# The opening of a recurrence and feed-forward layer kernel, rearranged: decay's row loaded alone ahead of x, clip logarithms on GpSimd, w2's absolute sums in halves, idle products ahead of x

## The chip, the cores and the metric

The kernel runs on one core of one Trainium2 chip. The metric is the device time of one execution in microseconds (us). The kernel before takes 821.13 us, the median of three runs (821.13, 821.13 and 821.78). Lower is better.

## The reference, cut to what matters

```python
def _L0_attn_ref(x, Wr, Wk, Wv, Wo, decay, ln_w):
    r = jax.nn.sigmoid(jnp.einsum('btd,ed->bte', x, Wr))
    k = jnp.einsum('btd,ed->bte', x, Wk)
    v = jnp.einsum('btd,ed->bte', x, Wv)
    log_decay = jnp.log(jnp.clip(jax.nn.sigmoid(decay), 1e-07))
    scale = jnp.exp(t * log_decay[None, :])               # t = 0 .. T-1
    cum = jnp.cumsum(k * v / jnp.clip(scale, 1e-10)[None], axis=1)
    y = _rmsnorm(r * cum * scale[None], ln_w)
    return jnp.einsum('btd,ed->bte', y, Wo)

def _L0_ffn_ref(x, w1, b1, w2, b2):                        # binarized: mean(|w|, axis=1) * sign(w)
    h = jax.nn.gelu(jnp.einsum('bsd,hd->bsh', x, bw1) + b1, approximate=False)
    return jnp.einsum('bsh,dh->bsd', h, bw2) + b2

x = _layernorm(x + _L0_attn_ref(x, ...))
x = _layernorm(x + _L0_ffn_ref(x, ...))                    # x: (8, 2048, 256), D = 256, H = 1024
```

## The kernel before

The 8 sequences of 2048 tokens are cut into 32 chunks of 512 tokens. A chunk passes through a pipeline of stages: x is scaled and split into two fp16 halves (xh on ACT, xl on DVE); R makes the products for k, v and r on PE (12 products of 512 columns for one half of the channels, one m at a time: m = 0 is k, 1 is v, 2 is r); kvs on DVE turns k and v into `kvg`; scans runs the recurrence along time and multiplies by r into `y`; ysq on ACT squares y, ysqs on GpSimd (POOL in the rows) adds the squares, block_sums on DVE and sum_rows on PE bring them to mean squares (mean_sq), and GpSimd takes the root (root_rms). yh and yl split y, O multiplies by Wo, residual1, ustats and norm1 make the first norm, F1 and gelu make the hidden layer, hh and hl split it (four pairs of 128-column blocks of the hidden layer in the first chunk), F2 makes the last product, and zmul, zadd, zstats and norm2 finish.

Five engines run five programs, each in the order in which its code is written, and meet at semaphores. Nothing is scheduled by a planner. Each program is a setup, a prologue and a loop. The loop runs the chunks; while PE does F2 of chunk i, the others prepare chunks i+1 to i+3. The setup and the prologue (the opening, up to the first F2 at about 58 us of the trace) prepare weights and bring the first chunks to their places in the pipeline. Only the opening is touched by the change.

What the opening does for the change:

- The DMA queue of SP loads the rows of decay, ln_w and b1 into one tile `rows` (L271 to L273), then x of chunk 0, the three projection weights, x of chunk 1, Wo, w1, w2 and more. PE transposes `rows` to columns (L556), DVE copies them (L1090), ACT takes the sigmoid and the logarithm of decay.
- The clip table `clip_g` holds, for each channel and time step, the factor that the clip at 1e-10 leaves: exp(min(t log d + 23.03, 0)). It is made in four parts of 512 steps. Parts 0 and 1: a product and a minimum on DVE (clip_logs, L1107) and an exponential on ACT (clip_table, L746). Parts 2 and 3: a rectified product on ACT (clip_excess, L734) and an exponential on ACT (L748).
- Weight scales: DVE takes the largest absolute value of a weight (proj_maximum, L1074), PE sums it over partitions (L480), DVE makes the scale (L1079, L1080), ACT splits the high half (proj_split_hi, L726), DVE the low half (proj_split_lo, L1084).
- The hidden layer's scale needs the sums of |w1| (alphas1, L766); the factor of the output needs the sums of |w2| (alphas2, L773), which DVE scales (L1173), GpSimd spreads over a diagonal (diagonal, L1316) and PE turns into a row (alpha2_to_row, L531).
- PE has a helper idle_products (L457): transposes of the identity whose result nobody reads.

## Time and profile before

| | |
|---|---|
| median of 3 runs | 821.13 us |
| the profiled execution's own time | 821.11 us |
| its span in the trace | 819.3 us |
| PE busy (matmul) | 798.8 us, 97% |
| DVE busy | 771.3 us, 94% |
| ACT busy | 679.9 us, 83% |
| POOL busy | 295.3 us, 36% |
| chain that ended last, by engine | PE 88%, DVE 4%, POOL 2%, ACT 2%, issue 2% |

The span is counted from the first record on the core. Between the profiled execution's time and its span lie 1.8 us, which the trace does not divide. A busy share is that of the whole span; the opening is 8% of it and has its own limits, so it is read from the timelines of the engines, in order of time, where a row says when an operation began, how long it took, and how long its engine was idle before it and who ended that.

### The profile page before, as it was taken

To read this page: it belongs to the slowest core of one execution; us is meant where nothing else is said; L and a number is where in the kernel's file an instruction comes from. 1 tells how busy PE (TensorE), PEld (TensorE's weight loads), DVE (VectorE), ACT (ScalarE), POOL (GpSimd) and SP (SyncE) were. 2 spreads that over 40 slices of the span, in tenths; PEclk is the share of its full clock that TensorE was granted. 3 is DMA by queue.
4 is the path that set the end of the run, shared out by engine and by line. 5 is a ranking of instruction groups with operands and counts; after the bars stand their busy time and mean duration, and the time that the engine had idled before them with its cause. 6 is when DMAs were issued, how large, how long until landed. Compare 5 with 4: busy or idle time off the path is not lost.

```text
span 819.3 us, 16575 instructions
## 1 busy us (share of the span) xinstructions
PE 798.8 (97%) x5174; PEld 505.7 (62%) x5174; DVE 771.3 (94%) x1472; ACT 679.9 (83%) x973; POOL 295.3 (36%) x572
## 2 busy tenths in 40 slices
PE   6989999999999999999999999999999999999986
PEld 4555666656666656666656666655666665666654
DVE  7998999999999999999999999999999999999887
ACT  7987888888888888888888888888888888887775
POOL 3343323344223344333344333344333334332344
PEclk9999999999999999999999999999999999999999
DMA  8513553434553434553434454444454344444313
GB/s 261 99 27 78 129 125 84 110 94 102 128 128 86 115 81 105 125 128 92 113 79 109 118 128 100 105 89 106 112 128 105 100 97 104 106 102 104 78 26 104
DMA packets 168286, 86.27 MB, mean 105 GB/s; under 512 B 128572, under 2 KB 163912, under 8 KB 168264
## 3 DMA queue, kind: packets, MB, share of 16 engines
q1 hardware_dynamic: 147288, 52.97, 27.5%
q0 software_dynamic: 4608, 16.78, 10.4%
q10 hardware_dynamic: 16368, 16.25, 5.6%
q8 instruction: 11, 0.18, 0.1%
q14 instruction: 11, 0.09, 0.0%
HBM read 20.45 MB, written 16.78 MB: 45 GB/s over the span
## 4 chain that ended last, share of the span: by engine, by line
PE 88%; DVE 4%; POOL 2%; ACT 2%; issue 2%; DMA 0%; SPq 0%; POOLq 0%; DVEq 0%; ACTq 0%
PE ps_r L375 28%; PE ps_o L496 26%; PE ps_f L446 19%; PE ps_r L446 6%; PE ps_o L401 6%; PE ps_o L406 3%; DVE hid_lo L1008 1%; DVE u L959 1%; ACT hid L678 1%; DVE u_st L967 0%; PE ps_s L383 0%; DMA x_in<-in_L_attn_x_dram 0%; POOL root L1322 0%; POOL y_sqs L1310 0%; DVE state L923 0%
## 5 line engine op out<-in xcount | busy, mean ns | idle before, releaser
L496 PE MATMUL ps_o<-w2T,hid_hi 128*128 128x256 f16 x992 | 218.9, 273 | 3.4 <-DVE hid_lo L1008 3.0
L496 PE MATMUL ps_o<-w2T,hid_lo 128*128 128x256 f16 x992 | 218.8, 272 | 0.0
L375 PE MATMUL ps_r<-x_t,proj_hi 128*128 128x512 f16 x768 | 197.1, 379 | 1.2 <-issue 0.7
L446 PE MATMUL ps_f<-x_t,w1T 128*128 128x512 f16 x768 | 181.7, 379 | 1.6 <-DVE x_t L992 1.3
L678 ACT ACTIVATE hid<-ps_f,rows_c,f_scale 128x512 f32<-128x512 f32 x192 | 145.2, 774 | 42.2 <-PE ps_f L446 37.1
L1008 DVE SCALAR_TENSOR_TENSOR hid_lo<-hid,hid_scale,hid_hi 128x1024 f16<-128x1024 f32 (+1 forms) x136 | 160.3, 1222 | 0.9 <-POOL hid_hi L1343 0.6
L1310 POOL TENSOR_TENSOR y_sqs<-y_sq 128x512 f32<-128x512 f32 x32 | 46.7, 1459 | 309.6 <-ACT y_sq L653 309.6
L375 PEld LDWEIGHTS ps_r<-x_t,proj_hi 128*128 128x128 f16 x768 | 74.7, 98 | 91.3 <-issue 2.8
L713 ACT ACTIVATE hid_hi<-hid,hid_scale 128x2048 f16<-128x2048 f32 (+2 forms) x72 | 127.9, 1778 | 3.2
L446 PEld LDWEIGHTS ps_f<-x_t,w1T 128*128 128x128 f16 x768 | 74.9, 98 | 79.7 <-issue 1.6
L375 PE MATMUL ps_r<-x_t,proj_lo 128*128 128x512 f16 x384 | 114.2, 379 | 0.2 <-DVE proj_lo L1084 0.2
L496 PEld LDWEIGHTS ps_o<-w2T,hid_hi 128*128 128x128 f16 x992 | 97.0, 98 | 20.2 <-DVE hid_lo L1008 5.9
L496 PEld LDWEIGHTS ps_o<-w2T,hid_lo 128*128 128x128 f16 x992 | 97.1, 98 | 14.4
L647 ACT ACTIVATE r_tanh<-ps_r,x_scl 128x512 f32<-128x512 f32 x64 | 43.9, 686 | 32.6 <-PE ps_r L375 29.4
L653 ACT ACTIVATE y_sq<-y 128x512 f32<-128x512 f32 x62 | 39.1, 630 | 37.0 <-ACT res L707 15.9
L446 PE MATMUL ps_r<-x_t,w1T 128*128 128x512 f16 x256 | 69.6, 378 | 0.0
L707 ACT ACTIVATE res<-res,z_shift,z_rstd 128x256 f32<-128x256 f32 x126 | 65.1, 589 | 4.8 <-POOL z_shift L1356 2.6
L1322 POOL TENSOR_TENSOR root<-ms,neg_half 128x4 f32<-128x4 f32 x32 | 32.8, 1024 | 93.0 <-DVE ms L949 93.0
L375 PEld LDWEIGHTS ps_r<-x_t,proj_lo 128*128 128x128 f16 x384 | 37.5, 98 | 45.7 <-DVE proj_lo L1084 0.9
L696 ACT ACTIVATE res<-u,u_shift,u_rstd 128x256 f32<-128x256 f32 x120 | 61.9, 588 | 1.7 <-POOL u_shift L1338 1.7
L923 DVE TENSOR_TENSOR_SCAN state<-decay_f,state,kvg 128x512 f32<-128x512 f32 x48 | 61.5, 1281 | 0.8
L401 PE MATMUL ps_o<-wo_lo,y_hi 128*128 128x256 f16 x248 | 59.2, 272 | 0.0
(191 smaller groups left out, 1332.2 us busy)
## 6 DMA issues: line engine op xcount, KB each, us to landing
x_in<-in_L_attn_x_dram SPq DMA_DIRECT2D x32, 512.0 KB, 4.1
res<-b_row POOLq DMA_DIRECT2D x32, 512.0 KB, 4.5
out_dram<-res ACTq DMA_DIRECT2D x31, 512.0 KB, 2.9
w_in<-in_L_ffn_w_dram SPq DMA_DIRECT2D x2, 1024.0 KB, 8.8
x_t<-x_st SPq DMA_TRANSPOSE x59, 3.7
b_row<-in_L_ffn_b_dram SPq DMA_DIRECT2D x1, 512.0 KB, 12.7
proj_in<-in_L_attn_Wk_dram SPq DMA_DIRECT2D x1, 256.0 KB, 3.8
proj_in<-in_L_attn_Wv_dram SPq DMA_DIRECT2D x1, 256.0 KB, 4.1
```

Source lines behind the costliest of these rows:

```text
L375: last = nc.tensor.matmul(ps_r[:, m, :], w[:, m, dc, ec * P:(ec + 1) * P], xx[:, :, dc, :], start=(n == 0), stop=(n == 3 * DC - 1))
L401: nc.tensor.matmul(dst[:, tt, :], y_hi[:, dc, tt * P:(tt + 1) * P], w[:, dc, :], start=(dc == 0 and n == 0), stop=False)
L446: last = nc.tensor.matmul(f1_bank[hc % NF], w1T[:, hc, dc, :], xx[:, :, dc, :], start=(dc == 0 and n == 0), stop=(dc == DC - 1 and n == 1))
L496: last = nc.tensor.matmul(o_tok[:, tt, :], hh[:, hc, tt * P:(tt + 1) * P], w2T[:, :, hc, :], start=(hc == 0 and n == 0), stop=(hc == HC - ...
L647: nc.scalar.activation(r_tanh[:, ec, :], ps_r[:, 2, :], ACT.Tanh, scale=x_scl[:, j, 4:5]).then_inc(s_r, 1)
L678: nc.scalar.activation(hid[:, hc, :], f1_bank[hc % NF], ACT.Gelu, bias=b1c[:, hc:hc + 1], scale=f1_scale[:, hc:hc + 1]).then_inc(s_gelu, 1)
L696: nc.scalar.activation(res[j][:, tt, :], u[:, tt, :], ACT.Identity, bias=u_shift[:, tt:tt + 1], scale=u_rstd[:, tt:tt + 1]).then_inc(s_x1, 1)
L707: nc.scalar.activation(res[j][:, tt, :], res[j][:, tt, :], ACT.Identity, bias=z_shift[:, tt:tt + 1], scale=z_rstd[:, tt:tt + 1]).then_inc( ...
L713: nc.scalar.activation(hid_hi[:, part, :], hid[:, part, :], ACT.Copy, scale=hid_scale[:, :]).then_inc(s_hh, part.stop - part.start)
L923: nc.vector.tensor_tensor_scan(state[j % 2][:, ec, :], decay_f[:, ec, :], kvg[:, ec, :], first, ALU.mult, ALU.add).then_inc(s_scan, 1)
L1008: nc.vector.scalar_tensor_tensor(out=hid_lo[:, part, :], in0=hid[:, part, :], scalar=hid_scale[:, :], in1=hid_hi[:, part, :], op0=ALU.mult ...
L1310: nc.gpsimd.tensor_tensor(y_sqs[:, :], y_sq[:, 0, :], y_sq[:, 1, :], ALU.add).then_inc(s_ysqs, 1)
```

## The change

1. decay's two rows go to a tile of their own, `decay_rows`, and are loaded first; x of chunk 0 is loaded second, the rows of ln_w and b1 behind it. PE transposes decay alone first and the others behind the transposes of x; DVE copies them in two pieces.
2. PE does 5 idle products before decay's transpose and 10 behind it, ahead of the transposes of x.
3. The clip logarithms of parts 1, 2 and 3 are made on GpSimd (clip_logs_pool); clip_logs(1) leaves DVE, both clip_excess and neg_log go. All exponentials use one form. clip_table(1) moves behind r_gates(0, 0, (0,)) on ACT, so proj_split_hi(2) follows proj_split_hi(1) directly; clip_table(2) and (3) move back too.
4. Wo's and ln_w's maxima move ahead of proj_split_lo(2) on DVE; take_xbound(1) goes between the two instructions of kvs(0, 0, 0).
5. alphas2 is done in two halves, one ahead of yh(1), one between the third and the fourth gelu of chunk 0; its scaling moves from DVE to GpSimd, and GpSimd's diagonal behind unscales(3, 3). The signs of w2 are taken before clip_table(3).
6. scans is divided into scan_state and scan_gate; for the first half of chunk 2 the gate goes behind all four hl of chunk 0. yl(1) goes ahead of block_sums(1), y_scale(1) ahead of ysqs(1), and sum_rows(1) on PE from the head of O(1) into it, behind its second low part. x1l_rows(1) goes ahead of the third pair of hl.

The core of the diff:

```diff
-            for row, w in ((0, decay), (DC, ln_w), (2 * DC, b1)):
-                n = HC if row == 2 * DC else DC
-                sp.dma_start(rows[row:row + n, :], w.rearrange("(c p) -> c p", p=P)).then_inc(s_rows_in, 16)
+            sp.dma_start(decay_rows[:, :], decay.rearrange("(c p) -> c p", p=P)).then_inc(s_decay_in, 16)
             load(0, 0, 0)
+            sp.dma_start(rows[0:DC, :], ln_w.rearrange("(c p) -> c p", p=P)).then_inc(s_rows_in, 16)
+            sp.dma_start(rows[DC:DC + HC, :], b1.rearrange("(c p) -> c p", p=P)).then_inc(s_rows_in, 16)
...
             def O(c, k, last_chunk=False):
-                if k < 2:
+                if k == 0:
                     sum_rows(c)
...
                 high(1)
                 low(1).then_inc(s_o, 1)
+                if k == 1:
+                    sum_rows(c)
                 low(2)
...
             def prologue():                                            # PE
                 pe.wait_ge(s_ident, 1)
-                pe.wait_ge(s_rows_in, 48)
-                nc.tensor.transpose(ps_rows, rows[:, :], ident[0:n, 0:n]).then_inc(s_rows_t, 1)
+                idle_products(ps_f[:, 1, :], 5)
+                pe.wait_ge(s_decay_in, 16)
+                nc.tensor.transpose(ps_decay, decay_rows[:, :], ident[0:DC, 0:DC]).then_inc(s_rows_t, 1)
+                idle_products(ps_f[:, 1, :], 10)
                 pe.wait_ge(s_x_in[0], 16)
...
                 transposes(x_bank[0][:, 0:DC, :], x_in[0], 0, (3,)).then_inc(s_tx, 1)
+                pe.wait_ge(s_rows_in, 32)
+                nc.tensor.transpose(ps_rows, rows[:, :], ident[0:n, 0:n]).then_inc(s_rows_t, 1)
...
             def prologue():                                            # ACT
                 proj_split_hi(1)
-                clip_table(1)
                 proj_split_hi(2)
                 xsq(1, 0, 1)
-                clip_excess(2)
                 r_gates(0, 0, (0,))
-                clip_table(2)
+                clip_table(1)
                 xh(1, 1, slot=1)
                 signs(w1_in, w1_sgn, s_w1_in, s_sgn)
-                xsq(2, 0, 2)
+                ysq(0, (0,))
                 r_gates(0, 0, (1,))
                 wo_split_hi()
-                ysq(0, (0,))
+                xsq(2, 0, 2)
                 ysq(0, (1,))
                 r_gates(1, 1, (0,))
-                clip_excess(3)
+                clip_table(2)
                 yh(0)
                 xh(2, 2, slot=2)
+                signs(w2_in, w2_sgn, s_w2_in, s_sgn2)
                 clip_table(3)
...
-                act.wait_ge(s_sgn2, 1)
-                alphas2()
                 x1h(0, 1)
                 ysq(1, (1,), y=y_second)
                 r_gates(2, 2, (1,))
+                alphas2((0,))
+                yh(1, y_second)
                 act.wait_ge(s_ready, 1)
-                gelu(0, range(0, 1))
-                yh(1, y_second)
-                gelu(0, range(1, 2))
+                gelu(0, range(0, 2))
                 act.wait_ge(s_ready, 2)
                 hh(0, pairs[0])
-                gelu(0, range(2, 4))
+                gelu(0, range(2, 3))
+                alphas2((1,))
+                gelu(0, range(3, 4))
...
             def diagonal():                                            # GpSimd
-                pool.wait_ge(s_hidden, 1)
+                pool.wait_ge(s_alpha, HC + DC)
+                pool.wait_ge(s_hread, 1)
+                nc.gpsimd.tensor_scalar(alpha2[:, :], alpha2[:, :], w_max[:, 5:6], 1.0 / (H * HTOP), ALU.mult,
+                                        ALU.mult).then_inc(s_alpha2, 1)
+                pool.wait_ge(s_alpha2, 1)
...
+            def clip_logs_pool(n, dcs=range(DC)):
+                pool.wait_ge(s_setup_a, 2)
+                part = slice(n * CH, (n + 1) * CH)
+                for dc in dcs:
+                    nc.gpsimd.tensor_scalar(clip_g[:, dc, part], steps[:, part], dec_c[:, 1, dc:dc + 1], -LOG_CLIP,
+                                            ALU.mult, ALU.min).then_inc(s_clip_pool, 1)
+            clip_logs_pool(1)
             pool.wait_ge(s_winv, 1)
             unscales(0, 0)
             def prologue():                                            # GpSimd
                 scales(1, 1)
                 unscales(1, 1)
+                clip_logs_pool(2)
+                clip_logs_pool(3, (0,))
                 ysqs(0)
                 y_scale(0)
                 y_unscale(0)
                 scales(2, 2)
                 unscales(2, 2)
+                clip_logs_pool(3, (1,))
                 root_rms(0)
                 root_u(0)
+                y_scale(1)
                 ysqs(1)
-                y_scale(1)
                 y_unscale(1)
                 scales(3, 3)
-                diagonal()
                 root_rms(1)
                 unscales(3, 3)
+                diagonal()
```

Three places where instructions moved on DVE. Names: `proj_in`, `wo_in` are weights as loaded, `w_inv` and `w_scl` scales, `x_st` and `x1_st` one name in the rows for staging tiles.

DVE in the setup, from the third projection's maximum on, before:

```order
L1107 TENSOR_SCALAR clip_g<-steps,dec_c 128x512 x2
L1084 SCALAR_TENSOR_TENSOR proj_lo<-ps_o,w_scl,proj_hi 128x512
L1079 TENSOR_SCALAR w_inv<-ps_s 128x1
L1080 RECIPROCAL w_scl<-w_inv 128x1
L1127 TENSOR_SCALAR w_inv<-w_inv 128x1
L1084 SCALAR_TENSOR_TENSOR proj_lo<-ps_f,w_scl,proj_hi 128x512
L907 SCALAR_TENSOR_TENSOR k_sb<-ps_r,x_scl,clip_g 128x512
L914 SCALAR_TENSOR_TENSOR kvg<-ps_r,x_scl,k_sb 128x512
L890 TENSOR_SCALAR x_scl<-ps_s 128x1
L1133 TENSOR_REDUCE w_max<-wo_in 128x1
L1135 TENSOR_REDUCE w_max<-rows_c 128x1
L923 SCALAR_TENSOR_TENSOR state<-decay_f,kvg 128x512
```

and now:

```order
L1088 SCALAR_TENSOR_TENSOR proj_lo<-ps_o,w_scl,proj_hi 128x512
L1083 TENSOR_SCALAR w_inv<-ps_s 128x1
L1084 RECIPROCAL w_scl<-w_inv 128x1
L1132 TENSOR_SCALAR w_inv<-w_inv 128x1
L1137 TENSOR_REDUCE w_max<-wo_in 128x1
L1139 TENSOR_REDUCE w_max<-rows_c 128x1
L1088 SCALAR_TENSOR_TENSOR proj_lo<-ps_f,w_scl,proj_hi 128x512
L904 SCALAR_TENSOR_TENSOR k_sb<-ps_r,x_scl,clip_g 128x512
L887 TENSOR_SCALAR x_scl<-ps_s 128x1
L911 SCALAR_TENSOR_TENSOR kvg<-ps_r,x_scl,k_sb 128x512
L919 SCALAR_TENSOR_TENSOR state<-decay_f,kvg 128x512
```

The two clip logarithms (L1107) are gone, the maximum of Wo (now L1137) and of ln_w stand ahead of the last proj_lo, and the bound of x (now L887) stands between k_sb and kvg.

DVE between the hidden scale and the first hid_lo, before:

```order
L1173 TENSOR_SCALAR alpha<-alpha,w_max 128x2
L923 SCALAR_TENSOR_TENSOR state<-decay_f,state,kvg 128x512
L926 SCALAR_TENSOR_TENSOR y<-r_tanh,state 128x512
L939 TENSOR_REDUCE y_part<-y_sqs 128x16
L932 SCALAR_TENSOR_TENSOR y_lo<-x_st,y_roots,y_hi 128x1024
L945 SCALAR_TENSOR_TENSOR ms_all<-ps_s,quarter 128x16
L949 TENSOR_REDUCE ms<-ms_all 128x4
```

and now:

```order
L919 SCALAR_TENSOR_TENSOR state<-decay_f,state,kvg 128x512
L936 SCALAR_TENSOR_TENSOR y_lo<-x_st,y_roots,y_hi 128x1024
L943 TENSOR_REDUCE y_part<-y_sqs 128x16
L949 SCALAR_TENSOR_TENSOR ms_all<-ps_s,quarter 128x16
L953 TENSOR_REDUCE ms<-ms_all 128x4
L1012 SCALAR_TENSOR_TENSOR hid_lo<-hid,hid_scale,hid_hi 128x1024
```

The scaling of alpha is gone from DVE, the gate that makes y is gone from behind the scan, and y_lo stands ahead of y_part.

DVE at the end of the opening, from norm1 of chunk 1 to the loop, before:

```order
L977 TENSOR_SCALAR res<-u,u_mv,u_rstd 128x256 x4
L1008 SCALAR_TENSOR_TENSOR hid_lo<-hid,hid_scale,hid_hi 128x1024 x2
L987 SCALAR_TENSOR_TENSOR x_st<-res,x_st 128x1024
L1008 SCALAR_TENSOR_TENSOR hid_lo<-hid,hid_scale,hid_hi 128x1024
L923 SCALAR_TENSOR_TENSOR state<-decay_f,state,kvg 128x512
L926 SCALAR_TENSOR_TENSOR y<-r_tanh,state 128x512
```

and now:

```order
L981 TENSOR_SCALAR res<-u,u_mv,u_rstd 128x256 x4
L1012 SCALAR_TENSOR_TENSOR hid_lo<-hid,hid_scale,hid_hi 128x1024
L991 SCALAR_TENSOR_TENSOR x_st<-res,x_st 128x1024
L1012 SCALAR_TENSOR_TENSOR hid_lo<-hid,hid_scale,hid_hi 128x1024 x2
L926 SCALAR_TENSOR_TENSOR y<-r_tanh,state 128x512
L919 SCALAR_TENSOR_TENSOR state<-decay_f,state,kvg 128x512
L926 SCALAR_TENSOR_TENSOR y<-r_tanh,state 128x512
```

The x_st of norm 1 (L987, now L991) moved ahead of the third hid_lo, and the gate (now L926) of the first half of chunk 2 stands behind the fourth.

## Rows read from the trace of the kernel before

**Rows 1.** Windows: span us, busy (instructions) of each engine, PE clock, DMA share, GB/s:

```profile
70.00:90.00 20.00, 20.00 (x131) 12.57 (x129) 19.54 (x38) 17.23 (x23) 7.20 (x16) 1.00 0.35 81
...
814.00:816.00 2.00, 0.00 (x0) 0.00 (x0) 0.78 (x4) 1.09 (x2) 0.89 (x3) 1.00 0.24 83
...
816.00:819.00 3.00, 0.00 (x0) 0.00 (x0) 0.73 (x2) 0.00 (x0) 0.16 (x1) 0.54 0.50 175
```

**Rows 2.** Timeline of PE, first F2 products: start us, us, operation, [idle before <-releaser]:

```profile
59.61 0.28 PE L496 MATMUL ps_o<-w2T,hid_hi 128*128 128x256 f16 x1 [0.80 <-DVE hid_lo L1008]
...
63.14 0.28 PE L496 MATMUL ps_o<-w2T,hid_hi 128*128 128x256 f16 x1 [1.29 <-DVE hid_lo L1008]
```

**Rows 3.** Timeline of DVE before the loop, last third of the opening:

```profile
45.50 0.15 DVE L901 TENSOR_SCALAR y_q<-y_q 128x1 f32<-128x1 f32 x1
...
46.02 0.24 DVE L1173 TENSOR_SCALAR alpha<-alpha,w_max 128x2 f32<-128x2 f32 x1
...
47.48 0.69 DVE L926 SCALAR_TENSOR_TENSOR y<-r_tanh,state 128x512 f32<-128x512 f32 x1
...
48.09 0.70 DVE L939 TRANSPOSE_TENSOR_REDUCE y_part<-y_sqs 128x16 f32<-128x512 f32 x1
...
48.72 1.24 DVE L932 SCALAR_TENSOR_TENSOR y_lo<-x_st,y_roots,y_hi 128x1024 f16<-128x1024 f32 x1
...
50.08 0.17 DVE L949 TENSOR_REDUCE ms<-ms_all 128x4 f32<-128x16 f32 x1
...
51.90 1.66 DVE L959 SCALAR_TENSOR_TENSOR u<-ps_o,rms,x_in 128x256 f32<-128x256 f32 x4
...
56.96 1.40 DVE L977 TENSOR_SCALAR res<-u,u_mv,u_rstd 128x256 f32<-128x256 f32 x4
...
61.81 1.27 DVE L1008 SCALAR_TENSOR_TENSOR hid_lo<-hid,hid_scale,hid_hi 128x1024 f16<-128x1024 f32 x1
```

**Rows 4.** Chain of waits, start us, us, what: the head:

```profile
1.17 0.25 SPq L273
...
1.78 3.61 DMA x_in<-in_L_attn_x_dram
```

**Rows 5.** Timeline of DVE, setup:

```profile
9.38 1.28 DVE L883 SCALAR_TENSOR_TENSOR x_t<-ps_r,x_scl,x_t 128x1024 f16<-128x1024 f32 x1
...
12.09 0.87 DVE L1107 TENSOR_SCALAR clip_g<-steps,dec_c 128x512 f32<-128x512 f32 x2
...
14.93 0.75 DVE L1084 SCALAR_TENSOR_TENSOR proj_lo<-ps_f,w_scl,proj_hi 128x512 f16<-128x512 f32 x1 [0.86 <-ACT proj_hi L726]
...
18.03 1.23 DVE L923 TENSOR_TENSOR_SCAN state<-decay_f,kvg 128x512 f32<-128x512 f32 x1
```

**Rows 6.** Timeline of ACT:

```profile
12.99 1.34 ACT L746 ACTIVATE clip_g<-clip_g,log_clip 128x512 f32<-128x512 f32 x2 [1.27 <-DVE clip_g L1107]
...
40.70 1.05 ACT L773 ACTIVATE w_in<-w_in 128x1024 f32<-128x1024 f32 x1
...
47.34 1.14 ACT L658 ACTIVATE y_hi<-x_st,y_roots 128x1024 f16<-128x1024 f32 x1
```

**Rows 7.** Timeline of PE, transposes at two rates, first hidden products and next sum:

```profile
5.43 1.54 PE L336 MATMUL ps_r<-ident,x_in 128*128 128x128 f32 x6 [2.25 <-DMA x_in<-in_L_attn_x_dram]
...
16.79 1.04 PE L336 MATMUL ps_o<-ident,x_in 128*128 128x128 f32 x8
...
45.55 1.89 PE L446 MATMUL ps_f<-x_t,w1T 128*128 128x512 f16 x8 [0.56 <-DVE x_t L992]
...
48.94 0.37 PE L383 MATMUL ps_s<-y_part,fold 128*128 128x16 f32 x2 [0.65 <-DVE y_part L939]
```

**Rows 8.** Timeline of POOL:

```profile
4.04 1.37 POOL L1395 TENSOR_SCALAR decay_f<-steps,dec_c 128x512 f32<-128x512 f32 x2 [0.43 <-DVE dec_c L1092]
...
46.05 0.70 POOL L1300 TENSOR_TENSOR y_roots<-y_q,halves 128x2 f32<-128x2 f32 x1
...
52.74 1.09 POOL L1295 DMA_DIRECT2D res<-b_row  x1 [0.46 <-issue]
```

77 lines of the change are left out of this document (35 added, 42 removed).

## The prediction, made before the changed kernel was run

> **What bounds the kernel now.** I read the windows by stage first. From 70 us on PE is busy for all 20.00 of 20 us, at full clock, with DVE at 19.54 [rows 1]; the page has PE at 97% of the span, and the chain that ended last is 88% PE. The diff touches nothing in the loop or behind it. So the change can only move the moment at which PE's unbroken stretch begins, and whatever it moves there goes into the end one for one. Next I read PE's timeline before the loop, for that moment. It is 63.14: PE has begun F2 of chunk 0 but waits for hid_lo on DVE, 0.80 us before 59.61 and 1.29 us before 63.14, and from there on it doesn't stop [rows 2]. The reader should see that the releaser is DVE each time. The fourth hid_lo starts at 61.81 on DVE [rows 3]. Going back through DVE's timeline, there is hardly an idle microsecond between 45 and 63, so the next question is what holds DVE there: work it need not do yet, and, at the single place where a wait counts (u at 51.90), GpSimd's root, which starts when `ms` is ready; from ms at 50.08 to u at 51.90 is 1.82 us [rows 3]. Further back lies the setup, where DVE waits 0.86 us for proj_hi on ACT, which stood behind a clip exponential for which ACT itself waited 1.27 us on DVE [rows 5, 6].
>
> Numbers below are the trace's times before, and by how much each comes earlier, which I call the lead.
>
> **Part 1, the head.** Before, SP issues three row loads and then x at 1.78, and x is there 3.61 us later, at 5.39 [rows 4]. Now x takes the slot of the second row load, 1.17. Issue and landing kept, x is there at 4.78, a lead of 0.61. The idle products fill a time in which PE has nothing: six transposes of this size took 1.54 us at 5.43 [rows 7], 0.26 each with the last one's tail and about 0.22 without, so 15 take 3.3 us; from about 1.8, when the identity is made (estimated from the start of GpSimd's work), they end at about 5.1. That is 0.3 us behind x, but the transposes of x don't set the next step: the squares of x on DVE do (they need 1.2 us), so PE's lateness is hidden as long as it is under about 0.5 us. The projection weights' load is not moved up and limits DVE's first maximum, which eats another 0.15. I take 0.45 of lead at xl (x_t on DVE, 9.38 before) [rows 5]; bounds 0.2 (all 0.3 us of lateness shows) and 0.61.
>
> Do the idle products make PE quick sooner? The eight transposes of x at 16.79 take 1.04 us where six at 5.43 took 1.54 [rows 7]: PE was on the lower of its two clocks (1.2 GHz) at 5.43 and on the higher (2.4 GHz) at 16.79. The granted clock column shows 1.00 in both, so only durations tell it. In this stretch DVE and ACT are the path, so a quicker PE gives at most the 0.34 us that DVE is idle before the first weight scale. I put it inside the bounds of the head.
>
> **Part 2, the setup.** Two things leave DVE's path between xl at 9.38 and the first scan at 18.03: the two clip logarithms of part 1 (12.09, until proj_lo can follow at 12.87: 0.80 us by starts, 0.87 by the row) and the wait of 0.86 for proj_hi(2), since ACT no longer does clip_table(1) first [rows 5, 6]. What hides the wait in its place: Wo's maximum (0.68) was behind kvg and now fills the time in which ACT makes proj_hi(2). Taking the bound of x between k_sb and kvg fills the 0.1 us in which kvg waits for k_sb's write. 0.80 + 0.86 + 0.1 = 1.76, so the scan starts at 18.03 - 0.45 - 1.76 = 15.8. The lead is 2.2. PE has to follow: its r product (m = 2) starts after proj_hi(2), 1.5 earlier, and it no longer waits for Wo's maximum (0.2 more, and 0.1 at the next k_sb), and another 0.4 in the wait at the first sum of bounds; so PE and DVE meet there with 2.2 each.
>
> The clip logarithms themselves go to GpSimd, six instructions. decay_f is the same form (one input of 128x512, one scalar per partition): 1.37 us for two, 0.69 each [rows 8]. Six are 4.1 us, in three places where GpSimd's timeline has it waiting for others, for 5.5 us (before the first unscales), 7.1 us (before the first ysqs) and 3.3 us (before the first root). I take zero on the path. From the other side: the nearest dearer row is y_sqs, two inputs, 1.49 us; at that price the three behind unscales(1) take 4.5 us and still end 2 us ahead of ysqs(0). The copy of the later rows adds about 0.1 on DVE where DVE was idle. ACT loses clip_excess twice (about 1.4 us each) and the two exponentials are only moved; ACT gets time between 15 and 45 us, none of which is on the path.
>
> From 18 to 45 us nothing else is changed that the path meets: clip_table(2) and (3) and w2's signs stay within ACT's freed time. The lead stays 2.2, and F1 starts at 45.55 - 2.2 = 43.35 [rows 7].
>
> **Part 3, from F1 to the fourth hid_lo.** Savings on DVE: the scaling of alpha (0.15 by starts, 46.02 to 46.17), the gate (0.69, now behind the fourth hid_lo) [rows 3]. But both are turned into waiting, and this is where I differ from a plain sum (2.2 + 0.69 + 0.15 = 3.0):
> - yq2 was made at 45.50 and is now at 43.3, ending 43.45; GpSimd's y_roots follows (0.70), then ACT's yh (1.14) ends at 45.4 [rows 3, 6, 8]. ACT has done the first alpha half (1.05) beside that. DVE's scan starts at 43.8, ends at 45.1; y_lo waits 0.3 and runs 45.4 to 46.6, y_part to 47.25.
> - On PE, the twelve products of F1 from 43.35 take 2.6 us (45.55 to 48.15 before) and O(1) starts at 45.95. sum_rows now stands behind eight high, two low, four high and two low products, 16 by 0.109 us = 1.75: 47.7. It was at 48.94, waiting 0.65 for y_part [rows 7], so its lead is 1.2. DVE gets the sum 0.35 us later, at 48.05, having waited 0.8; ms starts at 48.25 against 50.08: a lead of 1.83.
> - The chain ms, root on GpSimd, u keeps its 1.82 us, so u starts at 50.07 against 51.90. DVE does the first hid_lo meanwhile and waits about 0.5.
>
> From u to the end of the fourth hid_lo DVE does the same work as before (u, stats, k_sb, kvg, res at 56.96, four less one hid_lo, x_st), 11.15 us, in another order [rows 3]. The fourth ends at 61.2 and PE begins its stretch at 63.14 - 1.85 = 61.3. GpSimd must do alpha, diagonal (1.1 together, estimated from 0.24 and 0.73) and the issue of x1b (0.46 + 1.09) [rows 8] between the root and u_ve: from 50.0 + 0.5 to 53.2, against u_mv ready at 53.55. It fits by 0.35. ACT's second alpha half fits behind the third gelu. The gate moved behind the fourth hid_lo costs DVE 0.69 at the loop's entry, where DVE waits for over 2 us at the sum of bounds; hidden.
>
> **Sum.** 0.45 + 1.76 - (2.2 - 1.85) = 1.85 us. By bounds: head 0.2 to 0.61; setup 1.3 (the proj_hi(2) wait half stays) to 1.9; the late part between -0.8 (u_ve late too) and 0 (no new wait). The profiled execution took 821.11 us (span 819.3, 1.8 beside it), practically the median of 821.13, so 821.13 - 1.85 = 819.3.
>
> **A rule that speaks against it.** The timeline of DVE has POOL's and DVE's work side by side without a visible stretch on DVE, though POOL's own small operations vary. The Trainium skill, "GPSIMD Engine Reference", section "Key points", says that GpSimd shares its SBUF interfaces with VectorE and contends with VectorE instructions in a two-port mode or with two SBUF inputs. The new clip logarithms would then meet scans and gates. By that rule the six of them would be slower; no row here shows how much for this form.
>
> **Rivals.**
> - *More is given back* (0.22). x1b's issue or alpha's operations on GpSimd take a half to one microsecond longer, u_ve and with it res come late, or contention stretches DVE's scans during the clip logarithms. For: only 0.35 us of slack at u_ve. Against: GpSimd's rows of 128x512 are steady. Lead 1.1: 820.0.
> - *Less is given back* (0.13). sum_rows isn't late because PE is further ahead, or the head gives 0.6 and the quick clock 0.3. Lead 2.5: 818.6.
> - *The clock falls* (0.05), the slower side. F2 starts at about 54.5 now with one pair ready. PE does 8 products (0.87 us), then waits for the second hid_lo until 57.7 (2.3 us idle), does 0.87, and waits 1.5 for the third. In the last part of the trace PE idled through 814 to 816 at 1.00, and 816 to 819 shows 0.54 [rows 1]: longer idling did bring the lower level. If it falls in this gap, PE runs at half speed as it did from 5.43 for about 5 us after it began, losing 2.5 us; if it stays down twice as long, 5 us. 1.85 - 2.5 to 1.85 - 5: 821.8 to 824.3, at 823.0 in the middle. [...]
> - *It doesn't do what it says* (0.05). DVE's slots are refilled elsewhere, e.g. hid_lo waits for ACT's hh since the alpha half stands between gelus; PE's stretch starts within 0.5 us of before: 820.9.
>
> **How the numbers follow.** Forecast 0.55 with its own range 818.9 to 819.8. 0.2% is 1.64 us, about what a measurement of this kernel can tell from no change, and the line lies at 819.49, so the forecast's own spread splits: 0.40 below, 0.15 above. Faster: 0.40 + 0.13 + 0.02 of the first rival = 0.55. Same: 0.15 + 0.20 + 0.05 + 0.01 = 0.41. Slower: 0.04. Range for 8 in 10: 818.4 to 820.6, from the second rival to most of the first.
>
> **What would show it.** x in at 4.8; first scan at 15.8; F1 at 43.35; sum_rows at 47.7 with DVE idle 0.8 before ms_all; u at 50.07; fourth hid_lo at 60.0; PE's last wait ending at 61.3, with gaps of 2.3, 1.5 and 0.4 before it. Wrong if the scan leads by less than 1.7, if DVE's clip-time scans exceed 1.4 us, if u_ve has no idle before it, or if PE's products after the gap take more than 0.12 us each.

## The result: slower, 825.39 us against 821.15 us

The changed kernel took 825.39 us (median of 6 runs, 824.24 to 826.38), the kernel before 821.15 us (6 runs, 821.10 to 821.78). The ratio is 1.0051 with a 95% interval of 1.0038 to 1.0064. I had forecast 819.3 with a range up to 820.6. The profiled execution took 824.24 us with a span of 822.4, so it is the fastest of the six; its mean granted clock (the share of TensorE's full speed, averaged over the span) is 0.996. The six lie between 0.993 and 0.996, where the kernel before has 0.997 to 0.999 in its executions. The trace shows the fastest execution, so what it holds explains 3.1 us and not the 4.2 between the medians.

The spans differ by 3.1 us. I place them by one row that both traces have once per chunk, PE's sum of bounds. The first of the loop stands at 69.24 before and at 70.64 now, 1.40 us later:

```profile
69.24 0.17 PE L474 MATMUL ps_s<-bounds,ones 128*128 128x3 bf16 x1
```

```profile
70.64 0.17 PE L478 MATMUL ps_s<-bounds,ones 128*128 128x3 bf16 x1
```

The distance to the next ones is the same in both, except for a step of 1.31 us at 143.55. From the last of them to the end it is 41.14 before and 41.53 now: 0.39. Together 3.10.

| lead over before, us | forecast | trace |
|---|---|---|
| x_t (xl) of chunk 0 | 0.45 | 0.17 |
| first scan | 2.2 | 1.83 |
| F1 of chunk 0 | 2.2 | 0.78 |
| ms of chunk 1 | 1.83 | -0.07 |
| u of chunk 1 | 1.83 | -0.81 |
| res of chunk 1 | 1.83 | -1.17 |
| sum of bounds, chunk 2 | 1.85 | -1.40 |
| end of the span | 1.85 | -3.10 |

The timeline of DVE after, in the order start, duration, instruction, idle before and its releaser, answers to [rows 3, 5]:

```profile
9.21 1.28 DVE L880 SCALAR_TENSOR_TENSOR x_t<-ps_r,x_scl,x_t 128x1024 f16<-128x1024 f32 x1 [0.36 <-ACT x_t L648]
16.20 1.23 DVE L919 TENSOR_TENSOR_SCAN state<-decay_f,kvg 128x512 f32<-128x512 f32 x1
...
27.07 1.28 DVE L919 TENSOR_TENSOR_SCAN state<-decay_f,state,kvg 128x512 f32<-128x512 f32 x1
28.89 0.69 DVE L926 SCALAR_TENSOR_TENSOR x_st<-r_tanh,state 128x512 f32<-128x512 f32 x1 [0.53 <-DVE state L919]
...
46.87 1.80 DVE L936 SCALAR_TENSOR_TENSOR y_lo<-x_st,y_roots,y_hi 128x1024 f16<-128x1024 f32 x1 [0.34 <-ACT y_hi L667]
48.60 0.70 DVE L943 TRANSPOSE_TENSOR_REDUCE y_part<-y_sqs 128x16 f32<-128x512 f32 x1
49.95 0.17 DVE L949 SCALAR_TENSOR_TENSOR ms_all<-ps_s,quarter 128x16 f32<-128x16 f32 x1 [0.65 <-PE ps_s L385]
50.15 0.17 DVE L953 TENSOR_REDUCE ms<-ms_all 128x4 f32<-128x16 f32 x1
50.24 1.28 DVE L1012 SCALAR_TENSOR_TENSOR hid_lo<-hid,hid_scale,hid_hi 128x1024 f16<-128x1024 f32 x1
52.71 1.66 DVE L963 SCALAR_TENSOR_TENSOR u<-ps_o,rms,x_in 128x256 f32<-128x256 f32 x4 [1.18 <-POOL rms L1332]
...
55.83 0.38 DVE L975 BATCH_NORM_AGGREGATE u_mv<-u_st 128x2 f32<-128x6 f32 x4 [0.15 <-DVE u_st L971]
...
58.13 1.08 DVE L981 TENSOR_SCALAR res<-u,u_mv,u_rstd 128x256 f32<-128x256 f32 x3 [0.43 <-POOL u_rstd L1340]
```

The reader should see three things. The first scan came as early as forecast within 0.4 (16.20 for 15.8). Of the wait behind the scan at 27.07 the releaser is DVE's own scan, which had ended 0.54 us before. And u waits 1.18 for GpSimd, though DVE had ms at 50.15. GpSimd's timeline, to be held against [rows 8]:

```profile
4.15 2.33 POOL L1401 TENSOR_SCALAR decay_f<-steps,dec_c 128x512 f32<-128x512 f32 x2 [0.56 <-DVE dec_c L1096]
8.27 4.10 POOL L1412 TENSOR_SCALAR clip_g<-steps,dec_c 128x512 f32<-128x512 f32 x2
17.78 7.08 POOL L1412 TENSOR_SCALAR clip_g<-steps,dec_c 128x512 f32<-128x512 f32 x3
29.73 2.00 POOL L1412 TENSOR_SCALAR clip_g<-steps,dec_c 128x512 f32<-128x512 f32 x1
...
45.62 1.97 POOL L1313 TENSOR_TENSOR y_sqs<-y_sq 128x512 f32<-128x512 f32 x1
50.40 2.00 POOL L1329 TENSOR_TENSOR root<-ms,neg_half 128x4 f32<-128x4 f32 x1 [1.16 <-DVE ms L953]
...
56.78 0.19 POOL L1338 TENSOR_SCALAR u_ve<-u_mv 128x4 f32<-128x4 f32 x1 [1.48 <-DVE u_mv L975]
```

Six clip logarithms take 13.2 us (2.0 to 2.4 each), not 4.1, and the root takes 2.00, not 1.02. u_ve, GpSimd's first step towards u_rstd, begins 0.95 behind the start of u_mv. The rows of the kernel before:

```profile
50.34 1.02 POOL L1322 TENSOR_TENSOR root<-ms,neg_half 128x4 f32<-128x4 f32 x1 [1.56 <-DVE ms L949]
50.52 1.28 DVE L1008 SCALAR_TENSOR_TENSOR hid_lo<-hid,hid_scale,hid_hi 128x1024 f16<-128x1024 f32 x1 [0.27 <-ACT hid_hi L713]
55.03 0.38 DVE L971 BATCH_NORM_AGGREGATE u_mv<-u_st 128x2 f32<-128x6 f32 x4 [0.15 <-DVE u_st L967]
55.63 0.19 POOL L1331 TENSOR_SCALAR u_ve<-u_mv 128x4 f32<-128x4 f32 x1 [1.79 <-DVE u_mv L971]
```

The root began ahead of the first hid_lo there, and u_ve 0.60 behind u_mv. PE's timeline before the loop, against [rows 2], and its one wait in the loop:

```profile
57.39 0.27 PE L500 MATMUL ps_o<-w2T,hid_lo 128*128 128x256 f16 x1
60.78 0.38 PE L500 MATMUL ps_o<-w2T,hid_hi 128*128 128x256 f16 x1 [3.12 <-DVE hid_lo L1012]
60.96 0.42 PE L500 MATMUL ps_o<-w2T,hid_lo 128*128 128x256 f16 x1
...
63.13 0.40 PE L500 MATMUL ps_o<-w2T,hid_hi 128*128 128x256 f16 x1 [0.47 <-DVE hid_lo L1012]
...
64.17 0.32 PE L500 MATMUL ps_o<-w2T,hid_lo 128*128 128x256 f16 x1
64.33 0.27 PE L500 MATMUL ps_o<-w2T,hid_hi 128*128 128x256 f16 x1
...
143.55 0.82 PE L450 MATMUL ps_f<-x_t,w1T 128*128 128x512 f16 x3 [1.14 <-DMA x_t<-x_st]
```

Products follow each other by 0.21 us between 60.78 and 64.2 and by 0.11 us elsewhere: PE was on the lower of its two clocks (1.2 GHz) behind an idle time of 3.12 us. The windows say the same in the granted clock, PEclk, the column behind the engines' busy times:

```profile
core 0: us, PE busy (x) PEld busy (x) DVE busy (x) ACT busy (x) POOL busy (x), PEclk, DMA share, GB/s
50.00:60.00 10.00, 7.47 (x48) 4.48 (x45) 8.10 (x22) 7.32 (x11) 6.19 (x12) 1.00 0.27 53
60.00:70.00 10.00, 8.74 (x62) 6.50 (x63) 8.56 (x9) 5.75 (x12) 1.49 (x1) 0.83 0.35 66
70.00:90.00 20.00, 20.00 (x125) 12.01 (x124) 18.66 (x39) 17.94 (x23) 7.31 (x16) 1.00 0.39 83
```

### The profile page after: what moved, and what is told of

Read it like the earlier page. It is cut to its first block, busy times and chain, and to the rows that moved or that the text cites. A ratio compares the mean times of both kernels' runs of the same rounds, so it can differ in the third digit from the quotient of the medians.

```text
span 822.4 us, 16607 instructions
## 1 busy us (share of the span) xinstructions
PE 802.1 (98%) x5190; PEld 507.5 (62%) x5190; DVE 771.8 (94%) x1470; ACT 678.2 (82%) x969; POOL 312.4 (38%) x577
## 4 chain that ended last, share of the span: by engine, by line
PE 87%; DVE 4%; POOL 3%; ACT 2%; issue 2%; DMA 1%; SPq 0%; POOLq 0%; ACTq 0%; DVEq 0%
PE ps_r L377 27%; PE ps_o L500 25%; PE ps_f L450 18%; PE ps_r L450 6%; PE ps_o L403 6%; PE ps_o L408 3%; DVE hid_lo L1012 1%; DMA x_t<-x_st 1%; ACT hid_hi L722 1%; DVE u L963 1%; ACT hid L687 1%; POOL root L1329 1%; DMA proj_in<-in_L_attn_Wk_dram 0%; DVE u_st L971 0%; PE ps_s L385 0%
```

## The experiments

Four theories stood after the first comparison: the clip logarithms (form or contention), the late order with the root, the clock, and waits that had nothing to do with either (DVE's 0.5 us stalls, the DMA in the loop). The kernel before took 821.08 to 821.18 us (medians) beside the experiments. Each line under "Measured" gives the median, the ratio to the kernel before and its 95% interval. Leads are against before.

**1. All clip work back on ACT.** Parts 1 to 3 as clip_excess (with Relu), as before for 2 and 3.

```
-            clip_logs_pool(1)            # and (2), (3, (0,)), (3, (1,))
                 proj_split_hi(1)
+                clip_excess(1)
...
+                clip_excess(2)
                 wo_split_hi()
...
+                clip_excess(3)
```

> The changed kernel, with the clip logarithms of parts 1 to 3 made on ACT as rectified products (as parts 2 and 3 were before), none on GpSimd. Theory A (GpSimd's clip logarithms and DVE's instructions with two inputs hold each other up, which costs the opening its lead): GpSimd's 128x512 scalar operations of 2.0 to 2.4 us vanish, F1 of chunk 0 starts about 1.0 to 1.3 us earlier than the changed kernel's 44.77 (43.5 to 43.8), and the time falls by 1 to 2.5 us from 825.4, to 823 to 824.4. Theory B (the order of the late part: sum_rows inside O(1), y_lo beside GpSimd's sum of squares, the root beside hid_lo) says F1 starts earlier but u gains little, time 824.5 to 825.5. Theory C (PE's lower clock after the 3.1 us gap is most of the loss): the gap is as long as before, so 825 or so, with the same scatter.

Measured: 824.13 (6 runs, 822.71 to 824.81), 1.0031 [1.0019, 1.0043]. The lead at F1 is 0.31 instead of 0.78, since y_q of chunk 0 comes only at 25.69; I put that down to the excess ahead of Wo's split, which this run doesn't show by itself. The loop begins at 71.52. y_lo still takes 1.79 and the root 1.99, so these are not the clip work's doing. There was no step in the loop.

**2. Clip work on GpSimd alone.** The kernel before, with parts 2 and 3 on GpSimd.

```
-                clip_excess(2)           # ACT; clip_excess(3) too
+            clip_logs_pool(2)            # GpSimd, ahead of unscales(0, 0)
...
+                clip_logs_pool(3)        # behind unscales(1, 1)
```

> The kernel before, with one part of the change alone: the clip logarithms of parts 2 and 3 on GpSimd instead of ACT (part 1 stays on DVE). Theory A: the four take 2.0 to 2.4 us each, DVE's gates and scans beside them get 0.1 to 0.5 us longer, and the time rises by 0.3 to 1.0 us, to 821.5 to 822.1. Against it: GpSimd has room for them (it waited 5.5 and 7.1 us there) and ACT is freed of 2.9 us, so the time stays 821.1 or falls by up to 0.3.

Measured: 822.46 (11 runs, 822.30 to 823.01), 1.0011 [1.0002, 1.0020]. The pairs take 4.09 and 4.08. The move of four of the six, alone, costs 1.3 us in the median. In the profiled execution (822.99) it is 0.6 at the loop's begin, 1.1 in a step of the sums of bounds near 777 (PE waits there 0.17 for a transpose and 0.57 for ACT's squares of y), and 0.2 behind the last.

**3. The late order back.** The changed kernel with the second sum of rows at O(1)'s head, block_sums ahead of yl, and ysqs ahead of y_scale.

```
-                if k == 0:
+                if k < 2:
                     sum_rows(c)
...
-                yl(1, y_second)
                 block_sums(1)
+                yl(1, y_second)
...
+                ysqs(1)
                 y_scale(1)
-                ysqs(1)
```

> The changed kernel, with the three orders of the late part put back together: sum_rows(1) at the head of O(1) on PE, block_sums(1) ahead of yl(1) on DVE, ysqs(1) ahead of y_scale(1) on GpSimd. Theory B: ms of chunk 1 is ready about 49.4 instead of 50.15, the root starts ahead of the first hid_lo and takes 1.0 instead of 2.0 us, u starts at 50.8 to 51.3 instead of 52.71, the gap of PE shrinks from 3.1 to under 2, the clock stays up, and the time falls by 1.5 to 3 us, to 822.4 to 823.9. Theory A alone would leave it at 825.

Measured: 823.26 (11 runs, 822.39 to 824.90), 1.0023 [1.0014, 1.0032]: 2.1 us back. ms stands at 48.64 instead of 50.15, the root takes 1.02, u stands at 51.30 (-0.81 became +0.60). PE's idle time shrank to 2.00. Eight products at full speed follow it, then a wait of 1.30, and then 17 products on the lower clock (from 62.06): the shorter gap didn't keep the clock up, though I had expected that. GpSimd's u_ve still begins 0.95 behind u_mv, and res still waits 0.43, though the root is quick here.

**4. The gap filled.** 30 instead of 8 idle products ahead of F2 of chunk 0.

```
-                idle_products(ps_s, 8)
+                idle_products(ps_s, 30)
```

> The changed kernel, with 30 instead of 8 idle products on PE ahead of the row of alpha and F2 of chunk 0 (22 more, 2.4 us). They don't move the fourth hid_lo on DVE, only shorten PE's gap from 3.1 to about 0.8 us. Theory C: PE's products behind the gap take 0.11 us each instead of 0.21, and the median falls from 825.4 by 1 to 2.5 us and scatters less. Against it: the low clock costs only 0.3 us in the profile, since DVE's fourth hid_lo at 64.2 ends last anyway; then 825.0 to 825.4.

Measured: 822.91 (11 runs, 822.51 to 824.32), 1.0022 [1.0013, 1.0031]: 2.5 us back in the median, by work that computes nothing. The trace shows what it replaced:

```profile
55.82 3.00 PE L461 MATMUL ps_s<-ident 128*128 128x128 f32 x26
60.87 0.28 PE L500 MATMUL ps_o<-w2T,hid_hi 128*128 128x256 f16 x1 [0.73 <-DVE hid_lo L1012]
63.22 0.28 PE L500 MATMUL ps_o<-w2T,hid_hi 128*128 128x256 f16 x1 [1.30 <-DVE hid_lo L1012]
```

No product takes over 0.28 us. But in the profiled pair the sum of bounds of chunk 2 gains only 0.12 (70.64 to 70.52), since most of the slow time lay inside a wait for hid_lo; that is what the theory against the clock said. The other 1.3 us between these two executions (824.24 and 822.80) is the step in the loop, which this one doesn't have. Of its 11 runs the eight with a clock of 0.997 or more took 822.5 to 823.3, the three at 0.995 took 824.1 to 824.3; the changed kernel has no run above 0.996.

So the median's 2.5 us are not the clock's alone. What the clock can cost, the trace of experiment 12's first kernel shows. Its order of work is that of the changed kernel and its gap is 3.12 too, but there the eight products behind the gap were quick and the slow ones came behind the next wait, from

```profile
63.16 0.40 PE L500 MATMUL ps_o<-w2T,hid_hi 128*128 128x256 f16 x1 [1.30 <-DVE hid_lo L1012]
```

on, 14 of them. Its sum of bounds stands at 71.52, 1.00 later than with 30 idle products. (The one execution of the changed kernel with two memsets more, experiment 11, took 824.87 and has 28 slow products, up to 67.5.) My estimate from these three traces is 1.0 to 1.2 us for the clock and 1.3 for the step. Whether the idle products prevent the step, or only happened to go with its absence, isn't shown: it is back in the next two experiments, which have idle products as well.

**5 and 6. Both mends; then the wait ahead of the scan.** Experiment 3 with 24 idle products; and the same with DVE's wait for r_tanh put back ahead of the scan.

```
+                dve.wait_ge(s_r, DC * c + ec + 1)        # in scan_state
...
-                dve.wait_ge(s_r, DC * c + ec + 1)        # in scan_gate
```

> The changed kernel with both mends of the last two experiments together: the second sum of rows at O(1)'s head with the block sums and y's squares ahead as before, and 24 instead of 8 idle products ahead of F2. Theory A (two separate losses: the clock that falls in PE's gap, and the late order that holds the root back): the losses add, PE's stretch begins at about 61.7 instead of 63.2 with no product over 0.15 us behind it, the mean granted clock is 0.997 or more in most runs, and the time is the one with 30 idle products (822.9) less 1.3 to 1.5: 821.5. Rival B (the order's loss is only the clock's, counted twice): 822.9 again, with PE's last wait ending at 63. Rival C (what is gained ahead of the loop is given back in the loop by waits for the DMA of the transposed rows): the sum of bounds of chunk 2 at 69.2 or before, but a step of over 25.5 us in the loop in most runs, 822.5.

> The same as the last, but with the wait for r_tanh ahead of the scan, as the kernel before has it, instead of between scan and gate. Theory A (the gate that waits for two semaphores costs 0.07 to 0.08 us each, which the loop hides, but the last chunk doesn't, and it is a part of the 0.4 us by which every kernel made from the changed one has a longer end): from the last sum of bounds to the end 41.15 instead of 41.55 and 0.4 us less in all, 821.1. In the setup the scan then waits for r_tanh itself; y of chunk 1 comes at the same time or later. Rival B (the end is longer for another reason, such as where the chunks' loads and the stores fall): 41.5 stays, 821.5.

Measured: 822.48 (822.25 to 822.65), 1.0013 [1.0004, 1.0023], and 822.22 (821.97 to 822.57), 1.0010 [1.0001, 1.0019]. All clocks are 0.997 or more. The loop begins 1.7 us earlier than in experiment 4 (68.85), but a step of 1.1 us near 142 is back, as rival C said, so the mends do not add up in the median. In experiment 6 the stall of 0.54 at y of chunk 1 is gone (0.3 earlier); the end stays 41.55, so Theory A was wrong on the tail.

**7. All mended.** Experiment 6 with the clip work on ACT, the second part ahead of the first r gate.

```
                 xsq(1, 0, 1)
+                clip_excess(2)
                 r_gates(0, 0, (0,))
```

> The last one with all clip work of parts 1 to 3 on ACT, as clip excess; that of part 2 stands where the kernel before has it, ahead of the first r gate, and not ahead of Wo's split. Theory A (GpSimd's long instructions beside DVE's cost both engines; ACT has the time): xl at 9.2 to 9.5, the first scan at 15.8 to 16.2, y_q of chunk 0 at 24.5, F1 at 43.8, so the stretch of PE begins at 60.5 to 61.0 and the time is 820.0 to 820.6, under the kernel before. Rival B (ACT then becomes the path between 16 and 26 us, as in the first experiment): y_q at 25.5, F1 at 44.8, 821.1 to 821.5.

Measured: 820.42 (11 runs, 820.11 to 820.66), 0.9988 [0.9979, 0.9997]. The first scan is 0.75 later than in the changed kernel (16.95), and y_q of chunk 0 comes at 25.45, as rival B has it; but at u of chunk 0 it is ahead of experiment 6 (34.13 against 34.28), and there is no step in the loop. u_ve is back at 0.60 behind u_mv and res doesn't wait.

**8. What a GpSimd instruction costs by itself.** Three measurements without the layer's work; the core of the second:

```
nc.gpsimd.tensor_scalar(o, src, col, -23.0, ALU.mult, ALU.min)   # the clip logarithm
nc.gpsimd.tensor_scalar(o, src, 0.0, col, ALU.mult, ALU.add)     # the form of decay_f
nc.gpsimd.tensor_scalar(o, src, col, -23.0, ALU.mult, ALU.add)
...
nc.gpsimd.tensor_scalar(o, src, 0.5, -23.0, ALU.mult, ALU.min)
```

> A measurement alone: the kernel does none of the layer's work. GpSimd does, seven times, two clip logarithms (128x512 fp32, one input, one scalar a partition) and one small power of 128x4; beside it DVE does nothing, 6 products of two SBUF inputs, 6 scans, 6 products of PSUM and SBUF, 6 fp32 products with a scalar, 6 maxima, and nothing again. Theory A (GpSimd and DVE hold each other up where DVE reads two SBUF inputs or runs in its quick mode): 0.69 us each beside nothing, 1.3 to 2.4 beside the products of two SBUF inputs, the scans and the fp32 products with a scalar, 0.69 beside the maxima; DVE's own instructions get longer by up to 0.1. Rival B (it is GpSimd alone, such as the form with a minimum as its second operation): over 1.3 us each in all seven, the first and the last too.

> A measurement alone, with none of the layer's work in it. GpSimd does 128x512 fp32 instructions, two of each form, alone: a product with a scalar per partition and a minimum (the clip logarithm), a constant product and an added scalar per partition (the form of decay_f), the product with an added constant, with a second product, a constant product with a minimum, and the product with a maximum; then the form of decay_f beside scans on DVE, the 128x4 power alone, beside hid_lo's form on DVE and beside scans, and the sum of two tensors alone, beside products of two SBUF inputs and beside hid_lo's form. Theory A (the clip logarithm is dear because of its minimum): 2.03 us with a minimum or maximum, 0.69 in the other forms. Rival B (it is dear because its first scalar comes from SBUF): 2.03 in all forms that begin with a product by a scalar per partition, 0.69 with the constant product and the minimum. For what stands beside DVE: decay_f's form 1.0 to 1.4 beside scans, the power 1.02 alone and 1.6 to 2.0 beside hid_lo's form and the scans, the sum 1.26 alone and 1.7 to 2.0 beside DVE.

The first showed, as its rival B had it, that contention was not the reason for the 2.0 us, though it adds to them: two clip logarithms took 4.06 with nothing beside them, 5.32 beside products of two SBUF inputs, 5.69 beside scans, 4.61 beside fp32 products with a scalar, 4.07 and 4.06 beside a PSUM input and maxima. GpSimd's timeline of the second:

```profile
4.52 4.07 POOL L71 TENSOR_SCALAR pool_out<-src,col 128x512 f32<-128x512 f32 x2 [2.71 <-DVEq L101]
8.79 1.37 POOL L73 TENSOR_SCALAR pool_out<-src,col 128x512 f32<-128x512 f32 x2 [0.19 <-DVEq L101]
10.35 1.46 POOL L75 TENSOR_SCALAR pool_out<-src,col 128x512 f32<-128x512 f32 x2 [0.19 <-DVEq L101]
11.99 1.36 POOL L77 TENSOR_SCALAR pool_out<-src,col 128x512 f32<-128x512 f32 x2 [0.18 <-DVEq L101]
13.53 3.91 POOL L79 TENSOR_SCALAR pool_out<-src 128x512 f32<-128x512 f32 x2 [0.17 <-DVEq L101]
17.62 4.07 POOL L81 TENSOR_SCALAR pool_out<-src,col 128x512 f32<-128x512 f32 x2 [0.18 <-DVEq L101]
```

In order: product and minimum, decay_f's form, product and sum, two products, constant product and minimum, product and maximum. The minimum or maximum alone makes 0.7 us into 2.0. Theory A of the second is shown, and my "decay_f is the same form" was wrong by the second operation. What stood beside DVE in the same measurement missed my figures: decay_f's form took 1.60 each beside scans (expected 1.0 to 1.4), the power 1.24 beside hid_lo's form and 1.08 beside scans (1.6 to 2.0), the sum 1.47 beside either form (1.7 to 2.0). These are means over two to four in a row.

**9. Who begins first.** GpSimd's 128x4 power and 128x512 sum beside one 128x1024 instruction of DVE.

```
nc.vector.memset(firsts[:, 1, n:n + 1], 1.0).then_inc(s_ready_v, 1)   # DVE begins: GpSimd waits for this
nc.vector.scalar_tensor_tensor(out=wide_h_out, in0=wide_a, scalar=c, in1=wide_h, ...)   # hid_lo's form
```

> A measurement alone, with none of the layer's work. GpSimd's 128x4 power and its 128x512 sum are each put beside one 128x1024 instruction on DVE, hid_lo's form (fp32 and fp16 in, fp16 out) or a product of two fp32 SBUF inputs, once with DVE's begun first and once with GpSimd's. Theory A (a GpSimd instruction that comes behind hid_lo's form stands until that has ended, as in the changed kernel root began 0.16 behind and ended 0.88 behind it): behind hid_lo's form the power takes 1.9 to 2.1 and the sum about 2.4; ahead of it, 1.0 and 1.3. Rival B (both run, only slower): 1.2 to 1.5 whoever begins. Beside the two fp32 inputs I expect 1.0 to 1.3 for the power whoever begins.

GpSimd's timeline; a releaser "DVE firsts" means that DVE began, and the last three rows shown are sums:

```profile
4.96 1.03 POOL L72 TENSOR_TENSOR pool_small<-smalls,half 128x4 f32<-128x4 f32 x1
6.39 1.97 POOL L72 TENSOR_TENSOR pool_small<-smalls,half 128x4 f32<-128x4 f32 x1 [0.41 <-DVE firsts L94]
8.56 1.01 POOL L72 TENSOR_TENSOR pool_small<-smalls,half 128x4 f32<-128x4 f32 x1
10.29 1.90 POOL L72 TENSOR_TENSOR pool_small<-smalls,half 128x4 f32<-128x4 f32 x1 [0.72 <-DVE firsts L94]
12.39 1.01 POOL L72 TENSOR_TENSOR pool_small<-smalls,half 128x4 f32<-128x4 f32 x1
13.85 1.26 POOL L76 TENSOR_TENSOR pool_out<-src 128x512 f32<-128x512 f32 x1
15.52 2.21 POOL L76 TENSOR_TENSOR pool_out<-src 128x512 f32<-128x512 f32 x1 [0.41 <-DVE firsts L94]
17.93 1.26 POOL L76 TENSOR_TENSOR pool_out<-src 128x512 f32<-128x512 f32 x1
```

And DVE's instruction beside the sum, DVE first and GpSimd first:

```profile
15.33 1.28 DVE L99 SCALAR_TENSOR_TENSOR wide_h_out<-wide_a,c,wide_h 128x1024 f16<-128x1024 f32 x1
18.01 2.27 DVE L99 SCALAR_TENSOR_TENSOR wide_h_out<-wide_a,c,wide_h 128x1024 f16<-128x1024 f32 x1 [1.40 <-POOL firsts L67]
```

In all of these but one, whoever comes second stands until the first is done; the exception is DVE's instruction begun just behind the power, which took 1.28 or 1.23, the same as when it begins first. The power behind DVE's instruction takes 1.97 (that one ended at 7.49, the power 0.87 later), ahead of it 1.01. It is the same for two fp32 SBUF inputs (1.90), where I had expected 1.0 to 1.3. GpSimd's sum, begun first, makes DVE's 1.28 into 2.27. The Trainium skill, "GPSIMD Engine Reference", section "Key points", says that the two share SBUF interfaces and contend where DVE has two SBUF inputs; the trace agrees, with 0.9 to 1.0 us for one meeting, and here the order of begin decides who pays.

**10. The head alone.** The kernel before with decay's row, x and the later rows in the new order, and the 15 idle products.

```
+            sp.dma_start(decay_rows[:, :], ...).then_inc(s_decay_in, 16)
             load(0, 0, 0)
+            sp.dma_start(rows[0:DC, :], ...)          # then b1's
...
+                idle_products(ps_f[:, 1, :], 5)       # 10 more behind decay's transpose
```

> The kernel before with only the head of the change: decay's row, then x, then the rows of ln_w and b1, their own transpose and copy, and 15 idle products ahead of x. All clip work, the order of the setup and the late order are as before. Theory A (x comes 0.6 earlier, but the first maximum waits for the weights, so that 0.15 to 0.2 reaches xl, and the copy of the later rows costs 0.1 where DVE waits): xl at 9.2, the first scan 0.2 earlier, u of chunk 1 0.2 earlier, 821.0. Rival B (the quick clock on PE that the idle products give shortens the weights' transposes too): xl and the scan 0.4 to 0.5 earlier, 820.7.

Measured: 821.63 (11 runs, 821.42 to 822.67), 1.0006 [0.9997, 1.0015]. The squares of x begin at 4.71 instead of 5.41, a gain of 0.70; then DVE waits 0.69 for Wk, x_t stands at 9.46 (0.08 later than before), and a stall of 0.54 comes at 28.18. The part I priced at +0.45 is worth nothing by itself.

**11. The stalls and DVE's program.** Two memsets of one column more at DVE's start, in the changed kernel and in the mended one.

```
+            nc.vector.memset(pad[:, 0:1], 1.0)
+            nc.vector.memset(pad[:, 1:2], 1.0)
             dve.wait_ge(s_rows_t, 1)
```

> The changed kernel with two memsets of one column more at the very start of DVE, where it waits for the rows anyway. Theory A (the stalls of 0.53 us at y of chunk 1 behind its scan and at the last z_mv, which come behind a write of DVE's own and are in every kernel made from the changed one though the code at the second is the same as before, are bound to the place of the instruction in DVE's program, which the change shifted by two): both stalls go or move, and from the last sum of bounds to the end it is 41.15 instead of 41.53. Rival B (they come from what the instructions wait for): both stay, 41.53. The rest as in the changed kernel, 824 to 826 us.

> The mended version (clip work on ACT, late order back, 24 idle products, wait ahead of the scan), which took 820.42, with the same two memsets at DVE's start. Theory A (place in the program): the last z_mv waits no longer, 41.15 from the last sum of bounds to the end, and 820.0. Rival B: 41.58 and 820.4 as it was.

Measured: 824.87 in a single run (its trace is read for places, not for its time), and 820.14 (11 runs, 820.03 to 820.28), 0.9987 [0.9978, 0.9996]. Both stalls are gone from their places in the changed kernel (one of 0.5 now stands at a z_mv in the loop, where it is hidden), and the end is 41.19 and 41.12 us behind the last sum of bounds. The last z_mv in the mended kernel of experiment 7 without and with the two memsets:

```profile
814.14 0.25 DVE L1062 BATCH_NORM_AGGREGATE z_mv<-z_st 128x2 f32<-128x6 f32 x2 [0.53 <-DVE z_st L1057]
```

```profile
813.61 0.25 DVE L1063 BATCH_NORM_AGGREGATE z_mv<-z_st 128x2 f32<-128x6 f32 x2
```

So the stall hangs on the place in the program, which is shown by two kernels in which nothing else was changed. That it is the loading of instructions is only likely: in the view of the DMA queues an instruction packet on queue 14 lies about 0.6 us behind the stalls (29.5 and 818.4 in the changed kernel, 814.8 here), and with the two memsets it lies at 812.0. In the kernel before, such packets at 28.75 and 813.0 have no stall beside them. The Trainium skill, "Runtime: NRT & Kernel Launch", section "Instruction fetch mechanics", says that each engine's instructions are fetched in blocks by its own DMA queue, with a cost that is mostly hidden; these traces have 22 such packets in a run, and a visible cost at one or two of them, 0.5 us each, if that is what the stalls are.

**12. The quick form on GpSimd.** The clip logarithms with an added zero in place of the minimum (the clip is left out), first in the changed kernel, then with all mends of experiment 11.

```
-                                            ALU.mult, ALU.min).then_inc(s_clip_pool, 1)
+                                            ALU.mult, ALU.add).then_inc(s_clip_pool, 1)
```

> The changed kernel with the clip logarithms where they are, on GpSimd, but with an added zero in place of the minimum: it leaves the clip out, to see what the form's price is worth. Theory A (the 2.0 us of each instruction keep GpSimd late for the scales, so that lead is lost between the first scan and y_lo of chunk 0; the late order and the clock are separate): the clips take 0.7 to 1.0 each, the lead of 1.8 at the first scan is kept to y_q of chunk 0 (24.7) and F1 begins at 44.0 instead of 44.77; root still 2.0 and the clock still falls, 824.5. Rival B (the form's price was hidden as I forecast, and the lead goes elsewhere): F1 at 44.7 to 44.8 and 825.4.

> The same quick form, with the late order back, 24 idle products, the wait ahead of the scan and the two memsets at DVE's start. It is the mended version except that the clip work stays on GpSimd. Theory A (with the form's price gone GpSimd is as good a place as ACT): 820.0 to 820.3. Rival B (any 128x512 instruction of GpSimd beside DVE costs, whatever its form): 821.3 or more, near the 822.2 of the same kernel with the minimum.

Measured: 825.00 (5 runs, 824.04 to 826.06), 1.0047 [1.0033, 1.0060], and 821.03 (11 runs, 819.75 to 821.28), 0.9995 [0.9986, 1.0004]. In the changed kernel the price of the form makes no difference: y_q of chunk 0 at 25.02 instead of 25.12, and F1 at 44.80 instead of 44.77. Theory A had F1 at 44.0 and is refuted; rival B holds. With the mends it is worth 1.2 us against experiment 6, some 0.4 of it the two memsets. The loop then begins as early as with the clip work on ACT (68.08 and 68.16), though u_ve is late again (0.96 behind u_mv, res waits 0.43), but a step near 141 us costs 1.0.

**13. The step in the loop.** Six one-column instructions more on ACT in the last kernel; five on GpSimd in the mended one.

```
+            for i in range(6):
+                nc.scalar.activation(pad_a[:, i:i + 1], ones_col[:, :], ACT.Exp)
...
+            for i in range(5):
+                nc.gpsimd.memset(pad_p[:, i:i + 1], 1.0)
```

> The mended version with the quick form of the clip logarithms on GpSimd (which leaves the clip out; 821.03), with six one-column instructions more on ACT behind its third table load, where it waits for 1.5 us. So ACT's program is as long as with the clip work on ACT. Theory A (the single wait of PE for the DMA of x1_t near 141 us hangs on the place of ACT's instructions, and so on their loads, beside that DMA): the step of the sums of bounds over 25.4 us is gone, 819.9 to 820.1. Rival B (it comes from the clip work on GpSimd, or from the moment at which the loop begins): the step of 1.0 us stays, 821.0.

> The mended version with the clip work on ACT (820.14), with five one-column memsets more on GpSimd ahead of its iota, so that its program is as long as with the clip work. Theory A' (the single wait hangs on the place of GpSimd's instructions): a step of about 1.0 us in the loop comes, 821.1. Rival: no step, 820.1 to 820.2 (x's ident and steps come up to 0.2 later).

Measured: 821.19 (10 runs, 820.00 to 821.53), 1.0000 [0.9990, 1.0009], and 820.09 (10 runs, 819.87 to 820.38), 0.9986 [0.9976, 0.9996]. The nine slower runs of the first (821.1 to 821.5) stay where they were; the profiled one, at 820.00, has no step, and the others have no trace. The length of ACT's and GpSimd's programs is not the reason. What makes PE wait once for the transpose of x1 stays open. All I can say is where it comes: in 7 of 10 profiled executions with clip work on GpSimd, at 140.7 to 144.6 us (an eighth, experiment 2, has its step of 1.1 near 777, and 0.57 of that is a wait for ACT), and in none of 6 with the clip work elsewhere.

## Why the prediction was wrong

The miss in the span is 4.95 us (1.85 forecast, -3.10 found). By place, 0.37 of lead was missing at the first scan, 1.05 went between it and F1, 1.22 more than forecast between F1 and u, 0.59 between u and the sum of bounds of chunk 2, 1.31 at the step in the loop and 0.39 in the tail. Of the four signs of being wrong, three stayed away (scan lead 1.83, scans of at most 1.31, 1.48 of idle before u_ve) and the fourth came: products of 0.21 behind the gap. Point by point, by its steps:

**Part 1** failed in size: 0.17 for 0.45. x came 0.7 earlier, even more than forecast, but "the weights' load limits DVE's first maximum, which eats another 0.15" was far too small. It ate 0.56 (the first maximum stands at 6.39, before at 6.56), and all of the gain in experiment 10. The idle products made PE quick sooner (four transposes of a weight took 0.63 at 7.53, before 1.10 at 8.23); they ended 0.8 behind x and not 0.3, which the wait for Wk hid.

**Part 2** was right, within 0.1: the wait for proj_hi(2) went, and Wo's maximum filled its place. The first scan has 1.83 for 2.2, of which 0.28 is the head's.

**"The clip logarithms ... 0.69 each ... I take zero on the path"** failed by a factor of three. decay_f has the shape but not the operations, and I treated a row with another second operation as a price. The other end that I took, 1.49, was too low too: the nearest dearer row was no bound. Yet by experiment 12 this wasn't what made the changed kernel slow; it only stopped the mended one from gaining. What does go with the clip work's place on GpSimd, whatever its form, in the kernels made from the changed one, is a late u_ve and, in most traces, the step in the loop.

**"The lead stays 2.2" until F1** failed: 1.83 became 0.78. 0.5 of that is the stall at y of chunk 1 (28.89), bound to the place in the program (experiments 6 and 11). 0.44 went before y_q of chunk 0, half of it in a y that took 0.92 instead of 0.69, and 0.12 in y_lo (1.37 instead of 1.24). Both stand beside clip logarithms on GpSimd; that these made them longer is likely by experiment 8, not shown.

**"The chain ms, root, u keeps its 1.82 us"** failed: it took 2.56. I had written that DVE does the first hid_lo meanwhile, as if that were free. Before, the root began at 50.34 and hid_lo at 50.52; now hid_lo began at 50.24 and the root at 50.40, so it stood behind it (experiment 9). It turned on 0.2 us. Ahead of that, ms itself lost 0.85, more than the 0.78 that was left: y_part now stands behind y_lo, and y_lo began while GpSimd did y_sqs and took 1.80 instead of 1.24. Experiment 3, with the old order, gives 1.5 of ms back. This is the largest single step, 1.6 us of lead between F1 and u.

**"It fits by 0.35" at u_ve** failed in its result and not by its terms. GpSimd's alpha, diagonal and issue took 0.26, 0.73 and 1.09, as forecast, and then GpSimd stood idle for 1.48. Still u_ve began 0.95 behind u_mv instead of 0.60, and res waited 0.43 for u_rstd. The late root isn't the cause, since experiments 3, 5 and 6 have a quick root and the same 0.43. It comes in each kernel made from the changed one that keeps the clip work on GpSimd, and in none with it on ACT (experiments 1, 7, 11, 13's second), nor in experiments 2 and 10, made from the kernel before. Why, stays open.

**The rivals.** "More is given back" (0.22) names a late u_ve and longer instructions beside GpSimd, and both came. But its terms (alpha and the issue longer, scans stretched) did not, and its 820.0 is 5.4 us off. Down to u, 2.64 of the lead at the first scan were lost, where it had 1.1. No rival had the late root, the step or the tail, and the measured time lies above all of them.

**The clock** (0.05) is a rival that happened too, as a slow stretch of 3.4 us in the trace. It cost 0.12 us there and an estimated 1.0 to 1.2 in the median (experiment 4), less than half of the 2.5 I gave as its lower price. I took the gap as 2.3; it was 3.12. I also misread [rows 1]: 814 to 816 was only part of an idle time. PE's last product there began at 812.23 and took 0.27, and the clock fell about 816.2, 3.7 us later:

```profile
816.00:816.25 0.25, 0.00 (x0) 0.00 (x0) 0.05 (x1) 0.00 (x0) 0.16 (x1) 0.96 0.08 29
816.25:816.50 0.25, 0.00 (x0) 0.00 (x0) 0.25 (x1) 0.00 (x0) 0.00 (x0) 0.50 1.02 365
```

Read rightly, those rows spoke against a fall behind 2.3 us. The experiments have it otherwise: it fell behind gaps of 2.00 and 1.30 (experiment 3), and stayed up behind 0.73 and 1.30 (experiment 4). That the rival came is therefore no merit of the reasoning behind it.

**"The change can only move the moment at which PE's unbroken stretch begins"** failed. The tail (0.39, shown to hang on the place in DVE's program) and the step in the loop (1.31, open) are 1.7 us from places that I had called out of reach of the change.

## What to carry to other kernels

An instruction's price is that of its engine, shape and operations together: look for the row with the same operations, and measure it if there is none. Where GpSimd and DVE both read SBUF, ask who begins first at every short GpSimd instruction on the path, since moving work by 0.2 us can turn 1.0 us into 2.0. And when a saving ahead of PE's unbroken stretch isn't carried through to its begin, it becomes an idle gap, behind which the clock can fall. And code that the diff doesn't touch isn't out of its reach: 1.7 us of the loss came from there.

The mended version (experiment 11) keeps the change's head and setup order, with the clip work on ACT, the late order of before, 24 idle products and the wait ahead of the scan. It took 820.14 us, 1.0 under the kernel before (821.15) and 5.2 under the changed one.

## What was not expected of the hardware

- GpSimd's 128x512 fp32 product with a minimum or maximum takes 2.0 us, with a sum or a second product 0.7.
- A GpSimd instruction begun behind a DVE instruction of two SBUF inputs stands until that has ended (1.0 to 1.97 us); a DVE instruction behind GpSimd's sum likewise (1.28 to 2.27). Behind the power, DVE's was not held up (1.28).
- Two instructions more at an engine's start moved a stall of 0.5 us out of the last microseconds of the program.
- PE fell to its lower clock behind an idle time of 3.12 us, at once (the changed kernel) or only behind the next wait of 1.30 (experiment 12), and behind 2.00 and 1.30 with eight products between (experiment 3). It did not fall behind 0.73 and 1.30 (experiment 4), and at the end of the kernel before it stayed up for 3.7 us of idling.
